# Constant fillers, quarter-split first LoRA products and the second half of x on ScalarE's queue in a two-sequence LoRA and expert FFN kernel

## The reference, cut to what matters

```python
def _L0_cond_ref(hidden_states, expert_ids, wi, wo, common_wi_a, common_wi_b, common_wo_a, common_wo_b,
                 experts_wi_a, experts_wi_b, experts_wo_a, experts_wo_b):
    x = hidden_states
    hidden_i = jnp.einsum('bsd,fd->bsf', x, wi)
    hidden_i += ALPHA * jnp.einsum('bsr,fr->bsf', jnp.einsum('bsd,rd->bsr', x, common_wi_a), common_wi_b)
    hidden_i += _expert_lora(x, expert_ids, experts_wi_a, experts_wi_b)
    hidden_i = jax.nn.relu(hidden_i)
    ...
    return hidden_o

    # _L0_ffn_ref: gate on the mean over tokens, top 2 of 8 experts
    for e in range(E):
        hmid = jax.nn.gelu(jnp.einsum('bth,hf->btf', hidden_states, w1[e]) + b1[e], approximate=False)
        y = jnp.einsum('btf,fh->bth', hmid, w2[e]) + b2[e]
        out = out + combine[:, e][:, None, None] * y
x = x + _L0_ffn_ref(_L0_cond_ref(x, itok_B_0_7, ...), ...)
```

## Time and profile before

| | us |
|---|---|
| median of 3 runs | 266.44 (266.25 to 267.05) |
| the profiled execution, own time | 265.94 |
| its span, first to last instruction | 264.2 |
| PE busy in it | 260.0 (98%) |
| DVE, ACT, POOL busy | 174.3, 174.8, 160.7 |

### The profile page before, as it was taken

One profiled execution on the slowest core, in us unless ns is written; L12 is line 12 of the kernel. 1 busy time (PEld: TensorE's weight loads), 2 busy tenths in 40 slices (PEclk: granted clock), 3 DMA queues, 4 the chain that ended last, 5 costly groups with the idle time before them and its releaser, 6 DMA issues.

```text
span 264.2 us, 3622 instructions
## 1 busy us (share of the span) xinstructions
PE 260.0 (98%) x1156; PEld 212.8 (81%) x1156; DVE 174.3 (66%) x284; ACT 174.8 (66%) x279; POOL 160.7 (61%) x192
## 2 busy tenths in 40 slices
PE   8999999999999999999999999999999999999995
PEld 4778888888878888888888888888888888888884
DVE  1882867376998636657594866658856567665665
ACT  3857365455466289888976887676777677774650
POOL 2267997933398977897549999456366366331100
PEclk9999999999999999999999999999999999999999
DMA  6987120201032102211202112203202206000004
GB/s 187 382 322 244 35 79 0 84 1 40 0 124 79 51 28 80 82 22 59 83 0 63 60 38 79 79 0 83 79 2 79 78 4 200 0 0 2 0 1 159
DMA packets 11139, 19.76 MB, mean 75 GB/s; under 512 B 2000, under 2 KB 2256, under 8 KB 10992
## 3 DMA queue, kind: packets, MB, share of 16 engines
q1 hardware_dynamic: 10544, 18.61, 21.5%
q10 hardware_dynamic: 576, 0.92, 1.0%
HBM read 17.43 MB, written 2.10 MB: 74 GB/s over the span
## 4 chain that ended last, share of the span: by engine, by line
PE 98%; DVE 0%; issue 0%
PE out_ps L762 16%; PE out_ps L759 16%; PE out_ps L758 16%; PE hid_ps L758 15%; PE hid_ps L759 14%; PE hid_ps L762 14%; PE hid_ps L959 2%; PE hid_ps L798 1%; PE out_ps L888 1%; PE hid_ps L802 1%; PE hid_ps L806 1%; PE hid_ps L910 1%; PE hid_ps L900 1%; DVE x_sb L1271 0%; DVE y_sb L1159 0%
## 5 line engine op out<-in xcount | busy, mean ns | idle before, releaser
L413 POOL TENSOR_TENSOR up_lo<-up_raw,up_hi 128x512 fp32r<-128x512 f32 x41 | 53.0, 1311 | 37.1 <-ACT up_hi L573 36.9
L758 PE MATMUL out_ps<-hid_hi,down_hi 128*128 128x512 f32 x190 | 74.0, 390 | 0.0
L762 PE MATMUL out_ps<-hid_hi,down_lo 128*128 128x512 f32 x190 | 74.0, 389 | 0.0
L759 PE MATMUL out_ps<-hid_lo,down_hi 128*128 128x512 f32 x190 | 74.0, 389 | 0.0
L758 PE MATMUL hid_ps<-act_hi,up_hi 128*128 128x512 f32 x166 | 64.9, 391 | 0.0
L759 PE MATMUL hid_ps<-act_lo,up_hi 128*128 128x512 f32 x166 | 64.7, 390 | 0.0
L762 PE MATMUL hid_ps<-act_hi,up_lo 128*128 128x512 f32 x166 | 64.6, 389 | 0.0
L605 ACT ACTIVATE hid_ps<-hid_ps,bias_sb 128x512 f32<-128x512 f32 x64 | 42.2, 659 | 29.1 <-DVE hid_ps L1080 18.0
L1054 DVE SCALAR_TENSOR_TENSOR hid_lo<-hid_ps,mix,hid_hi 128x512 fp32r<-128x512 f32 x64 | 47.9, 748 | 20.3 <-ACT hid_hi L619 19.7
L419 POOL TENSOR_TENSOR down_lo<-down_raw,down_hi 128x512 fp32r<-128x512 f32 x24 | 32.4, 1349 | 37.2 <-ACT down_hi L583 37.2
L619 ACT ACTIVATE hid_hi<-hid_ps,mix 128x512 fp32r<-128x512 f32 x64 | 44.1, 690 | 4.7
(11 more groups left out here) (98 smaller groups left out, 241.9 us busy)
## 6 DMA issues: line engine op xcount, KB each, us to landing
up_raw<-in_w SPq DMA_DIRECT2D x16, 256.0 KB, 2.8
down_raw<-in_w SPq DMA_DIRECT2D x16, 256.0 KB, 2.6
lora_raw<-in_lora SPq DMA_DIRECT2D x10, 256.0 KB, 4.8
down_raw<-in_woT SPq DMA_DIRECT2D x8, 256.0 KB, 3.8
up_raw<-in_wiT SPq DMA_DIRECT2D x7, 256.0 KB, 4.2
outT<-x_sb SPq DMA_DIRECT2D x6, 256.0 KB, 3.5
x_sb<-in_x1T SPq DMA_DIRECT2D x1, 1024.0 KB, 7.6
x_sb<-in_x0bT SPq DMA_DIRECT2D x1, 512.0 KB, 4.0
```

The costliest lines, as they stand in the source:

```text
L413: ins = eng.tensor_tensor(up_lo[:, n, cols], up_raw[:, n, cols], f32(up_hi[:, n, cols]), ALU.subtract)
L758: eng.matmul(out, w_h, a_h, start=start, stop=False, skip_group_check=onto)
L759: eng.matmul(out, w_h, a_l, start=False, stop=False, skip_group_check=onto)
L762: return eng.matmul(out, w_l, a_h, start=False, stop=stop, skip_group_check=onto)
```

## The change

It has five parts.

1. **Fillers.** PE no longer waits for DVE's zeros. The fillers read a constant (bfloat16 1.0, one column repeated) that POOL writes before the five streams start. Ten fillers are issued in place of 12, and one more stands between the raw products of set 0 and those of set 1. DVE's clearing is 128 columns in place of 256.
2. **Raw LoRA products.** `lora_first` is now 128 partitions by 384 columns: set 0 uses partitions 0 to 63 and set 1 partitions 64 to 127, and the two products of a set read different quarters of 32 partitions and write different PSUM banks. Each set has its own load (64 partitions by 384 columns, 96 KB) with its own semaphore. The signal for the merge of set 0 comes once, after both products. The expert's number is read without its bounds.
3. **x on ScalarE's queue.** `load_x0(1)` moves from SP to ACT, behind ACT's two other loads and ahead of ACT's first computing instruction, and `x0_high(1)` moves up ahead of `up0_high`.
4. **First set.** `merge0` and `up0_high` go in pieces of 128, 128 and 256 columns; `first_pair` becomes `first_half` and `second_half` with the same 24 matmuls in another order. DVE's `merge_up(1)` moves behind its last `x0_low`, and PE waits for it ahead of `down_factor(0)`.
5. **LoRA rows.** Of lots (0, 0) and (0, 2) only the half that is read is split, so ACT copies 256 columns in place of 512 and POOL has one piece in place of two, in each.

The core of the diff:

```diff
-    WARM_UP = 12
+    WARM_UP = 10
-        zeros = y_sb[:, 0, 0:TOK // 2].bitcast(BF16)
-        lora_first = sb("lora_first", [G, LOT + SW])
+        lora_first = sb("lora_first", [P, P + SW])
+        def parts(b, lot):
+            return {(0, 0): [0], (0, 2): [1]}.get((b, lot), [0, 1])
+        FIRST_COLS = [slice(0, P), slice(P, SW), slice(SW, 2 * SW)]
...
+            def load_first(n, e):
+                rows = slice(2 * n * G, 2 * (n + 1) * G)
+                eng.dma_start(lora_first[rows, :], early[bass.ds(e, 1), n, :, :].rearrange("e r c -> (e r) c"))\
+                   .then_inc(s_lora_first[n], 16)
-            e = number(ids[0:1, 0:1])
-            eng.dma_start(lora_first[:, :], early[bass.ds(e, 1), :, :].rearrange("e r c -> (e r) c"))\
-               .then_inc(s_lora_first, 16)
-            load_x0(eng, 1)
+            e = eng.value_load(ids[0:1, 0:1])
+            load_first(0, e)
+            load_first(1, e)
             eng.dma_start(x_sb[:, 0, 1, :, :], x0bT[:, :, :]).then_inc(s_x0b, 16)
...
             load_x0(eng, 0)
             load_up(eng, 0)
+            load_x0(eng, 1)
             x0_high(0)
+            x0_high(1)
             up0_high(0)
             up0_high(1)
-            x0_high(1)
+            up0_high(2)
...
+            def first_half():
+                eng.wait_ge(s_x0hi, 1)
+                for f in range(2):
+                    eng.wait_ge(s_up0hi, f + 1)
+                    first_one(0, f, 0, False, False, start=True)
+                    if f == 0:
+                        eng.wait_ge(s_x0lo[0][0], 1)
+                    first_one(0, f, 0, False, True)
+                eng.wait_ge(s_up0lo, 1)
+                for f in range(2):
+                    first_one(0, f, 0, True, False)
+                eng.wait_ge(s_x0hi, 2)
+                eng.wait_ge(s_up0hi, 3)
...
-            def raw_up_factor(q, *outs):
-                eng.wait_ge(s_lora_first, 16)
-                own = block(1 + q, SW)
+            def raw_up_factor(q):
+                eng.wait_ge(s_lora_first[q], 16)
                 for kd in range(KD):
-                    ins = eng.matmul(outs[kd], lora_first[:, block(kd)], lora_first[:, own], start=True, stop=True)
-                    if q == 0:
-                        ins.then_inc(s_prod0, 1)
-                if q:
-                    ins.then_inc(s_prod, 1)
+                    rows = block(2 * q + kd, G)
+                    ins = eng.matmul(out_ps[:, 2 * q + kd, 0:SW], lora_first[rows, 0:P], lora_first[rows, P:P + SW],
+                                     start=True, stop=True)
+                ins.then_inc(s_prod if q else s_prod0, 1)
...
-            eng.wait_ge(s_zero, 1)
             warm_up(WARM_UP)
-            raw_up_factor(0, out_ps[:, 0, 0:SW], out_ps[:, 1, 0:SW])
-            raw_up_factor(1, out_ps[:, 2, 0:SW], out_ps[:, 2, SW:2 * SW])
-            first_pair(0)
-            first_pair(1)
+            raw_up_factor(0)
+            warm_up(1)
+            raw_up_factor(1)
+            first_half()
+            second_half()
+            eng.wait_ge(s_merge, product_count("u", 1))
             down_factor(0, out_ps[:, 3, :])
```

More of the change, by code:

```diff
@@ L184, in build @@
         s_x0b, s_x1 = sem("s_x0b"), sem("s_x1")
-        s_lora_first = sem("s_lora_first")
+        s_lora_first = [sem(f"s_lora_first{n}") for n in range(2)]
         s_up_raw = [sem(f"s_up_raw{n}") for n in range(NU)]
@@ L556, in lora_high, with up0_high @@
                     eng.wait_ge(s_prod, product_count("d", lot - 1))
[L557 to L562, removed]
+                eng.activation(lora_st[:, to], lora_raw[0:LR, raw], ACT.Copy).then_inc(s_lhi, 1)
+            def up0_high(n):
+                eng.wait_ge(s_merge0, n + 1)
+                cols = FIRST_COLS[n]
                 eng.activation(up_hi[:, 0, cols], up_raw[:, 0, cols], ACT.Copy).then_inc(s_up0hi, 1)
@@ L788, in first_low, with first_one @@
                 return up_lo_made(q)
-            def first_pair(t):
+            def first_one(t, f, kd, low_w, low_a, start=False, stop=False):
+                w, a = (up_lo if low_w else up_hi), (act_lo if low_a else act_hi)
+                return eng.matmul(hid_ps[:, 2 * t + f, :], w[:, 0, block(kd * 2 + f)], a[:, 0, kd * NT + t, :],
+                                  start=start, stop=stop)
+            def first_half():
[11 more added lines that the diff above has]
+                eng.wait_ge(s_up0hi, 3)
+                for f in range(2):
+                    first_one(0, f, 1, False, False)
+                eng.wait_ge(s_x0lo[1][0], 1)
+                for f in range(2):
+                    first_one(0, f, 1, False, True)
+                eng.wait_ge(s_up0lo, 2)
+                for f in range(2):
+                    first_one(0, f, 1, True, False, stop=True).then_inc(s_up, 1)
@@ L800, in first_pair @@
                     for f in range(2):
[L801 to L808 removed]
+                        first_one(1, f, kd, True, False)
@@ L810, in plain_tile @@
+                for kd in range(KD):
+                    eng.wait_ge(s_x0lo[kd][1], 1)
+                    for f in range(2):
+                        ins = first_one(1, f, kd, False, True, stop=(kd == KD - 1))
+                        if kd == KD - 1:
+                            ins.then_inc(s_up, 1)
             def plain_tile(q, j):
@@ L1032, in up0_low, with in_shape, merge_up @@
                                   ALU.subtract).then_inc(s_up0lo, 1)
-            def merge_up(q, bank):
-                w = up_raw[:, q % NU, 0:4 * P]
+            def in_shape(w, product):
+                return w.rearrange("p (k c) -> p k c", c=SW) if len(product.shape) == 3 else w
+            def merge_up(q, product):
+                w = in_shape(up_raw[:, q % NU, 0:4 * P], product)
                 eng.wait_ge(s_up_raw[q % NU], 16 * (q // NU + 1))
                 eng.wait_ge(s_prod, product_count("u", q))
-                eng.scalar_tensor_tensor(out=w, in0=bank, scalar=ALPHA, in1=w, op0=ALU.mult, op1=ALU.add)\
+                eng.scalar_tensor_tensor(out=w, in0=product, scalar=ALPHA, in1=w, op0=ALU.mult, op1=ALU.add)\
                    .then_inc(s_merge, 1)
```

62 lines of the change are left out of this document (32 added, 30 removed).

## The result

The changed kernel is slower, by 0.9%. Its median over 6 runs is 269.51 us (267.67 to 269.92), against 266.89 us (266.25 to 267.42) of the kernel before in 6 runs beside it; the ratio of the runs is 1.0087, with a 95% interval of 1.0054 to 1.0121. The forecast was 266.1 with a range of 265.5 to 266.9.

The account below looks back on a forecast made before the run. PE bound the kernel: a fixed run of matmuls behind a 7.15 us start. Raw load 4.9 plus products 2.04 gave 6.94, -0.21 on the profile (265.73); for the median 266.44 - 0.35 = 266.1 us, range 265.5 to 266.9.

Parts of the forecast that it names:

- Fillers from about 0.8: Start of PE: without the wait for the zeros, fillers begin at 0.87 us in place of 1.20.
- Issue of the LoRA rows at 2.65: SP's queue: without the two register instructions of the bounds, the load is issued at about 2.65 us.
- The load of the raw rows: LoRA load ahead of PE's raw products: lands at 4.75 us, plus 0 to 0.35 for x, 0.15 taken; PE begins at 4.9.
- The second pair's load: Set 1's LoRA rows: landed by about 5.4 us, PE asks at 6.1, so hidden with 0.7 us to spare.
- 12 long fillers suffer more than ten: Fillers when the clock rises 1 us later: a gain of 0.5 us, so 0.35 taken for the median.
- The sum for a rows' landing at 5.2: Rival at the LoRA load: rows share the engines with x, 0.3 of the gain is gone, 266.4 us; chance 0.13.
- The raw products, 2.04 with overlap: PE from first raw load to first tile: three steps per pair in place of four, 2.04 us; before, 1.92.
- The rival without overlap: Raw products: two pairs in a row cost 0.43 us more, first tile at 7.37, about 266.5 us; chance 0.25.
- A border costs 0.3: PE between full-height and 32-partition matmuls: about 0.31 us from last start to next weight load.
- What I called hidden: First tiles: x's earlier copy, ACT's third issue and PE's wait for `merge_up(1)` cost nothing.
- POOL's narrow margin: POOL's `up_low(1)` ahead of its use by PE: margin falls from 0.3 to about 0.05 us; cost 0 to 0.1, 0 taken.
- The slower rival: ACT before the first tile: x's copy holds up `up0_high`, first matmul at 7.55, +0.4 us, 266.9; chance 0.07.

Follow-up runs that it names:

- e7: The kernel before, with its 12 fillers reading the constant and not waiting for the zeros: median 266.09 against 266.55 us, ratio 0.9978.
- e2: The changed kernel with x's second half back on SyncE's queue and its copy back behind the high parts: median 265.67 against 266.4 us, ratio 0.9962.
- e11: e2 run again unedited, against the kernel before: median 265.84 against 266.62 us, ratio 0.9981.
- after: The profiled execution of the changed kernel, the fastest of its first six runs: own time 267.67 us, against 265.94 for the kernel before.
- e15: The changed kernel again, no edit, for another profile: own time 268.35 us.
- e1: The changed kernel with 17 fillers in place of 10: median 267.2 us against 266.4 for the kernel before, ratio 1.0019.
- e4: The kernel before with 6 fillers in place of 12, nothing else: median 269.64 us, ratio 1.0111.
- e12: The changed kernel again, no edit, for another profile: own time 265.76 us.
- e6: e2 without the filler between the two raw pairs: median 265.61 us over 9 runs, ratio 0.9987 to the kernel before.
- e14: The changed kernel again, no edit, for another profile: own time 269.37 us.
- e5: The changed kernel again, no edit, for a second profile: median 267.9 us over 10 runs, ratio 1.0005; profiled own time 269.52 us.
- e13: The changed kernel again, no edit, for another profile: own time 267.50 us.
- e10: e2 with both sets' LoRA rows in one load with one semaphore: median 267.37 us, ratio 1.0004 to the kernel before.
- e8: The changed kernel with x's second half still on ScalarE's queue but issued behind the first activation, its copy behind the high parts: median 267.71 us, ratio 1.0030.
- e9: e2 with 12 fillers in place of 10: median 266.19 us, ratio 0.9976 to the kernel before.
- e3: The kernel before with x's second half loaded from ScalarE's queue as its third load, no longer from SyncE's: median 267.12 us, ratio 1.0039.

## Why the prediction was wrong, point by point

- **Fillers from about 0.8.** Right: 0.78. That they were what came last ahead of the raw products was right too (e7).
- **Issue of the LoRA rows at 2.65.** Right: 2.61.
- **The load of the raw rows, landing at 4.75 plus 0 to 0.35.** Failed, and this is the first step that did. It landed at 5.91, and in the other profiles between 5.44 and 5.94: 0.7 to 1.2 us late where I had taken 0.15. Of that, 0.3 isn't x's doing, since without x in the way it lands at 5.05 and 4.99 (e2, e11), not at 4.75. The rest, 0.4 to 0.9, comes with x. I had priced x as if all 16 signals of the load came later by the same 0.15. The eighth does come only 0.18 to 0.59 later than in e2, in the six profiles, but PE waits for the last. The Trainium skill, "DMA: Bandwidth & Descriptors", section "Issuing engines are not separate DMA queues", says that such loads interleave on the same 16 engines. The traces agree as to the direction; my upper end, 0.35, was still below all that was measured, and even it I had set aside. The range for PE's start, up to 5.25, was cut off with it.
- **The second pair's load, "hidden, with 0.7 us to spare".** Failed: the second rows landed at 6.27 in the profile after, 0.9 behind the 5.4 that I had, but at 7.5 in e15 and 7.8 in e1, where PE then waited 0.54 and 0.74 for them.
- **The clock.** This step is missing, and it is the larger one: I put at nothing what a gap does to the steps behind it. I had used the clock for the fillers alone, and only as a gain ("12 long fillers suffer more than ten"). The sum put the raw products at 4.9 behind a tenth filler that starts at 4.35; any later landing would leave PE idle, and I priced the idle time at itself. e4 shows what six fillers fewer and their gap are worth: 3.2 us with nothing else changed. In the changed kernel the clock costs 0 to 3.7 us, by run. The sum for a rows' landing at 5.2, "266.4", should have read: 266.4 if the clock stays up.
- **The raw products, 2.04 with overlap.** Too high. Both records of a product run beside those of the other one, not only the second beside the first. Narrow windows of the timeline after (5.955 to 5.96, and 6.5 to 6.7):

```profile
5.95 0.48 PE L927 MATMUL out_ps<-lora_first 32*128 32x256 f32 x2 [1.47 <-DMA lora_first<-in_early]
...
6.27 0.38 PE L927 MATMUL out_ps<-lora_first 32*128 32x256 f32 x2
```

  The first two start by 5.96, the last two at 6.27: a pair takes two steps, not three, and the whole block 1.61 us where the clock is up (e12). The rival without overlap fell. The Trainium skill, "TensorE: Matmul & The Clock Gate", Part 3, puts the cost of issuing each further tile at about 4 ns. The trace agrees: a window that ends at 5.955 holds one of the two, and one that ends at 5.96 both; their recorded starts are 6 ns apart.
- **A border costs 0.3.** Right: 6.27 to 6.59 to 6.91.
- **What I called hidden.** Right. x landed at 5.73, its copy was done when ACT came to `up0_high`; no wait shows at set 1, and from the first tile to `down_factor(0)` e2 takes 5.60 us where the kernel before takes 5.65. POOL's narrow margin cost nothing.
- **The slower rival** had x holding up ACT's copies, at +0.4, with a chance of 0.07 and 0.06 for slower in all. The mechanism that decided was another, and none of the rivals had it.
- **The range** of 265.5 to 266.9 is where the kernel lies when its clock stays up, 5 of 16 runs. As the median's range it was wrong.

What is not settled: why the clock rises at 3.6 us in one execution, at 4.3, 5.9 or 6.5 in another, after fillers that begin at 0.78 in all of them, and what exactly decides whether a gap costs it. e6 had a gap of 0.44 and kept its clock, e14 one of 0.28 and did not get it before 13.5. The traces show nothing in the kernel that differs between them. Side by side the profiles show an order, which no run tests. Where PE went idle while its steps were still long (e4, e5, e14), they stayed long up to 13.4 to 13.6. Where the clock had risen first, it fell at 7.0 to 8.6 behind an idle stretch of 1.24 to 1.47 us (after, e13, e10) or two that add up to 1.3 to 1.4 (e8, e15), and stayed up over 0.69 and 0.74 (e12, e1); in e6 it rose within the gap. With no gap at all it rose by 6.8 (e9) at the latest.

**The version to keep** is e2: the change without its third part. It is faster than the kernel before (0.9962, and 0.9981 with an interval that just reaches 1) and than the changed kernel, and none of its 24 runs falls into the upper heaps.

## What to carry to other kernels

Before you shorten a row of fillers, or start it earlier with fewer of them, find out when the data behind it lands at its latest, and let the fillers reach that far: two fillers too many cost at most some tenths of a us here (e9, 0.35 between the medians), six too few cost 3.2. A small load that the start of the kernel waits for should have the DMA engines to itself; a large load that "only" uses another queue is not priced by the share that it takes on average: the small load is there when the last of its signals is, and here that one moved by 0.4 to 0.9 us. And where a clock is involved look at every run, not at the median of a few: a kernel with three heaps of times has a cause that one profile doesn't show.

## What the runs showed of the hardware

- Behind six fillers and a gap of 1.29 us PE stayed at the clock's lower level for the next 8 us of unbroken work (e4: steps of 0.43 from 5.23 to 13.4). Once fallen, at 7.0, the clock came back at 10.4 (after) or 13.9 (e8).
- The same kernel with the same landing time ran 3.6 us apart by the clock alone (e12, e14).
- Moving 256 KB from behind a 96 KB load to a second queue ahead of it raised that load's time from 2.1 to 3.1 us (e3), and in the changed kernel the first one's from 2.35 (e2) to 3.3 (2.7 to 3.3 in its six profiles). With the 96 KB load the eighth of its 16 signals moved by 0.19 us and the last by 0.86 (e2, after).
- Two fp32 products on different quarters of the partitions run wholly side by side, both records of each.
- With one 192 KB load split by partitions into two of 96 KB the first half landed 0.9 us earlier (5.05 against 5.93); the 256 KB load behind them was then also issued 0.95 us later, and no run parts the two (e2, e10).
